# Graph network layers on one core: the attention layer's sum over edges as an inner loop of two groups, with a mask table of two groups

## What is computed

```
h = h @ W_lin + b_lin ; feat = (h @ W_gat).reshape(N, 8, 32)
el = sum(feat * attn_l, -1) ; er = sum(feat * attn_r, -1)
e = leaky_relu(el[src] + er[dst], 0.2)
m = segment_max(e, dst) ; e = exp(e - m[dst]) ; s = segment_sum(e, dst)
out = segment_sum(feat[src] * (e / s[dst])[:, :, None], dst)
```

## Time and profile before

| | us |
|---|---|
| median of 3 runs (4096.9 to 4102.8) | 4097.34 |
| the profiled execution's own time | 4102.93 |
| its span, first to last instruction | 4101.1 |
| PE busy (share of the span) | 2926.9 (71%) |
| DVE busy | 1751.3 (43%) |
| POOL busy | 1369.7 (33%) |
| ACT busy | 884.6 (22%) |
| PE products L2202, 832 rows | 232.1 |
| POOL gathers L1974, 416 | 406.9 |
| PE's mean granted clock, share of full speed | 0.849 |

### The profile page before, as it was taken

The page is one execution under the profiler, slowest core; times in us unless marked ns, Lnnn a source line. Parts: engine busy times, 40 slices in busy tenths (PEclk is TensorE's granted clock), DMA queues, the critical chain, the costliest instruction groups (busy, mean ns, idle before and its releaser), DMA issues. The chain is left out here.

```text
span 4101.1 us, 44629 instructions
## 1 busy us (share of the span) xinstructions
PE 2926.9 (71%) x13021; PEld 2101.9 (51%) x13087; DVE 1751.3 (43%) x4387; ACT 884.6 (22%) x1236; POOL 1369.7 (33%) x980
## 2 busy tenths in 40 slices
PE   2888779624344454779999979999999997434445
PEld 1455568423233333546666657989883443223334
DVE  5876445436556456733333314434343222111214
ACT  0246643100000000112222224444431221000000
POOL 2122200255554450037777740000000001666663
PEclk9999889756666667889999989999999999666767
DMA  1157875233332220122222227666743444333332
GB/s 56 61 201 248 289 263 163 86 93 87 95 94 87 81 82 26 39 78 74 74 74 74 77 67 264 199 210 206 267 133 112 141 141 140 93 91 92 91 90 88
DMA packets 325254, 504.89 MB, mean 123 GB/s; under 512 B 27225, under 2 KB 238877, under 8 KB 317005
## 3 DMA queue, kind: packets, MB, share of 16 engines
q1 hardware_dynamic: 284477, 391.28, 28.4%
q0 software_dynamic: 40672, 112.31, 9.9%
HBM read 351.56 MB, written 152.75 MB: 123 GB/s over the span
## 5 line engine op out<-in xcount | busy, mean ns | idle before, releaser
L1854 POOL DMA_INDIRECT e7got<-rel_d,rel_i x416 | 396.0, 952 | 1212.6 <-POOLq L2645 1013.8
L1974 POOL DMA_INDIRECT a_got<-feat_d,src_i x416 | 406.9, 978 | 594.3 <-POOLq L2303 238.6
L1488 PE MATMUL s_aggs<-s_blk_r,high 128*128 128x512 f32 (+1 forms) x1050 | 400.5, 381 | 21.0 <-DVE low L1607 20.8
L1488 PE MATMUL s_aggs<-s_blk_r,low 128*128 128x512 f32 (+1 forms) x1050 | 389.1, 371 | 0.0
L2686 PE MATMUL q_prods<-w,q_xt 128*128 128x512 f32 x800 | 352.6, 599 | 13.4 <-ACT q_xt L2706 13.4
L1890 PE MATMUL e7sums<-e7got,e7hot 128*128 128x256 f32 x832 | 257.7, 468 | 141.8 <-issue 121.8
L1706 POOL TENSOR_SCALAR g_absent<-g_pairs 128x3200 bf16<-128x3200 f32 x25 | 274.9, 10995 | 171.7 <-DMA g_pairs<-pairs_d 171.7
L1862 DVE TENSOR_SCALAR e7hot<-iota,dloc,weight 128x128 f32<-128x128 f32 x416 | 115.9, 364 | 480.1 <-DMA g_pairs<-pairs_d 356.7
L1753 PE MATMUL g_sums<-value,g_turned 128*128 128x257 f32 x1250 | 298.8, 383 | 8.6 <-ACT g_turned L1817 8.6
L1890 PEld LDWEIGHTS e7sums<-e7got,e7hot 128*128 128x128 f32 x832 | 195.7, 240 | 203.1 <-issue 168.7
L1731 PE MATMUL g_scores<-key_t,g_q 128*128 128x512 f32 (+1 forms) x700 | 280.4, 556 | 20.6 <-DMA g_q<-query_d 13.4
(11 more groups left out here) (416 smaller groups left out, 4513.2 us busy)
## 6 DMA issues: line engine op xcount, KB each, us to landing
s_blk<-turned_d SPq DMA_DIRECT2D x60, 1280.0 KB
rel_d<-q_rows SPq DMA_DIRECT2D x25, 2048.0 KB
s_blk<-turned_d SPq DMA_DIRECT2D x45, 960.0 KB
pairs_d<-u_rows SPq DMA_DIRECT2D x25, 1600.0 KB, 8.1
turned_d<-u_line SPq DMA_DIRECT2D x25, 1600.0 KB, 7.1
g_pairs<-pairs_d SPq DMA_DIRECT2D x25, 1600.0 KB, 6.8
t_blk<-pairs_d SPq DMA_DIRECT2D x20, 1280.0 KB
t_blk<-pairs_d SPq DMA_DIRECT2D x15, 960.0 KB
```

Source lines behind the costliest of these rows:

```text
L1488: last = pe.matmul(aggs[:, idx % 2, half, 0:w], feats[l][part][:, a, half * P:(half + 1) * P], blk_r[:, q % RINGS, a % GA, 0:w], start=a = ...
L1854: pool.indirect_dma_start(got[:, j % U, :], None, table, bass.IndirectOffsetOnAxis(ap=index[:, j:j + 1], axis=0)).then_inc(arrived[j % U / ...
L1974: pool.indirect_dma_start(got[:, n % 2, s, :], None, table, bass.IndirectOffsetOnAxis(ap=k.src_i[:, j:j + 1], axis=0)).then_inc(arrived[n ...
```

## The change

The eight groups of `total` become an inner loop on TensorE of four passes with two groups each. The group's word is loaded in the pass, just ahead of the group's waits, and the eight loads at the start of a chunk go. The slot of `got` is now addressed by a register. `hot` shrinks from 32 slots to 8, two groups, which are used in turn; so the mask of a group has to wait for the products of two groups earlier, not of the chunk before. `turn(n + 1)` moves from between groups 5 and 6 to behind group 7.

```diff
-        hot = sb("hot", [P, CS, P])
+        hot = sb("hot", [P, 8, P])
...
                 for g in range(NG):
-                    if n >= 1:
-                        dve.wait_ge(multiplied, (n - 1) * NG + g + 1)
-                    j = n * CS + 4 * g
-                    dve.tensor_tensor(hot[:, 4 * g:4 * g + 4, :], spreads[:, 256:256 + P].unsqueeze(1).broadcast_to([P, 4, P]),
+                    if n * NG + g >= 2:
+                        dve.wait_ge(multiplied, n * NG + g - 1)
+                    j, m = n * CS + 4 * g, 4 * (g % 2)
+                    dve.tensor_tensor(hot[:, m:m + 4, :], spreads[:, 256:256 + P].unsqueeze(1).broadcast_to([P, 4, P]),
                                       k.dloc[:, j:j + 4].unsqueeze(2).broadcast_to([P, 4, P]), ALU.is_equal).then_inc(made, 1)
...
-                def multiply(g, u):
-                    ins = pe.matmul(sums[:, 0:W], hot[:, 4 * g + u, :], got[:, b, 4 * g + u, :], start=False, stop=False)
-                    if u == 3:
-                        ins.then_inc(multiplied, 1)
-
-                for g in range(NG):
-                    if more and g == NG - 2:
-                        turn(n + 1, 1 - b)
-                    word = words[g]
-                    pe.wait_ge(made, n * NG + g + 1)
-                    pe.wait_ge(weighed, n * NG + g + 1)
-                    with pe.If((word & 15) == 0):
-                        for u in range(4):
-                            multiply(g, u)
...
+                def multiply(m, u, group):
+                    slot = (group * 4 + u).with_bounds(min_val=0, max_val=CS - 1)
+                    return pe.matmul(sums[:, 0:W], hot[:, 4 * m + u, :], tile_of(got[:, b, :, :], slot), start=False, stop=False)
+
+                with pe.Fori(0, NG // 2) as i:
+                    for m in range(2):
+                        g = i * 2 + m
+                        word = load_word(pe, k, (n * NG + g).with_bounds(min_val=0, max_val=S // 4 - 1))
+                        pe.wait_ge(made, n * NG + g + 1)
+                        pe.wait_ge(weighed, n * NG + g + 1)
+                        with pe.If((word & 15) == 0):
+                            for u in range(4):
+                                last = multiply(m, u, g)
+                            last.then_inc(multiplied, 1)
...
+                if more:
+                    turn(n + 1, 1 - b)
                 zeros(False).then_inc(closed, 1)
 
             def chunk(n, b, more):
-                words = [load_word(pe, k, n * NG + g) for g in range(NG)]
                 maximum(n, b, more)
-                total(n, b, more, words)
+                total(n, b, more)
```

More of the change, by code:

```diff
@@ L2192, in zeros, with total @@
                 return pe.matmul(sums[:, 0:W], k.zero_b[:, 0:P], k.zero_b[:, 0:W], start=start, stop=not start)
-            def total(n, b, more, words):
+            def total(n, b, more):
                 pe.wait_ge(resumed, n + 1)
@@ new lines, in total @@
+                with pe.Fori(0, NG // 2) as i:
[8 more added lines that the diff above has]
+                            last.then_inc(multiplied, 1)
+                        with pe.If((word & 15) != 0):
+                            for u in range(4):
+                                with pe.If(turn_here(word, u) != 0):
+                                    zeros(False).then_inc(full, 1)
+                                    pe.wait_ge(copied, tile_before(word, u) * 2 + 2)
+                                    zeros(True)
+                                last = multiply(m, u, g)
+                            last.then_inc(multiplied, 1)
```

## The result

The changed kernel takes 4166.62 us (median of 4 runs, 4157.39 to 4170.99), the kernel before 4100.07 us in the runs beside it (4 runs, 4096.90 to 4103.27): 1.0159 times the time, 95% interval 1.0139 to 1.0179, that is 66.5 us slower. The forecast was slower, by 45. The profiled execution took 4166.38 us with a span of 4164.6, 63.5 more than that of before.

The account below looks back on a forecast made before the run. Taken as the bound: waits for PE signals passed late during POOL's gather bursts. 37 + 27 = 64.0 us against 60.4 gave +40 over 11 chunks, chunks 11 and 12 +5: +45, 4142 us, range 4075 to 4225.

Parts of the forecast that it names:

- What bounds the kernel: Attention chunks with gathers: PE's signals pass late during POOL's bursts; nearly 19 us of waiting per chunk.
- Loads out of the start: Eight word loads, 5.1 us, leave each chunk's start; mostly free, a gain of 3.8 us once was taken.
- The mask's wait and late signals: DVE's masks wait for products two groups back; with late signals the scan comes 37 us after POOL's restart, against 32.2.
- Chunks 11 and 12: The last two attention chunks, without gathers beside them: +3 and +2 us, together +5.
- The loop: PE's inner loop: 39 branches back cost 8 us of sequencer time, already counted, without fetch stalls.
- R: Theory set up for the experiments: the loop's register steps cost the time; mask table and `turn`'s place don't matter.
- A: Rival, faster: early breaks in POOL's bursts bring the scan 25.2 us after restart; 4025 us, or 4064; chance 0.13.
- C: Rival, hardly a change: the burst's end releases the scan as now, 34.3 at most; 4097 to 4105 us; chance 0.15.
- D: Rival: each of 39 inner branches back stalls PE 4.7 us, +183, some hidden; 4280 us; chance 0.03.
- B: Rival, slower still: DVE hears of groups 4 and 5 only at the burst's end; 4201 to 4223 us; chance 0.24.

Follow-up runs that it names:

- e9: Kernel before with `turn` moved to the head of `total`, ahead of the carried sum: 4069.84 us, ratio 0.9976.
- e6: Pair, kernel before and changed kernel, both without three of every four gathers from chunk 2 on: 3733.40 us (0.9941) and 3834.48 us (1.0202).
- e0: Kernel before, unchanged, run once more for its trace on a second chip: 4083.14 us in one execution.
- e4: Kernel before with only the load of the word moved into the group: 4089.25 us, ratio 1.0022.
- e3: Kernel before with only `turn` moved behind group 7: 4129.24 us, ratio 1.0125.
- e2: Kernel before with only the mask table of two groups: 4101.09 us, ratio 1.0058.
- e1: Kernel before with two-group mask table, word load in the group and `turn` behind group 7, but no loop: 4121.96 us, ratio 1.0108.
- e5: Changed kernel with `turn` put back between groups 5 and 6, the last pass written out: 4132.51 us, ratio 1.0131 to the kernel before.
- e8: Changed kernel with a four-group mask table and two loop passes of four groups: 4146.45 us, ratio 1.0179 to the kernel before.
- e7: Kernel before with a POOL fill of some 2 us ahead of every fourth gather from chunk 2 on: 3896.68 us, ratio 1.0371.
- e11: Kernel before with `turn` at the head of `total` and word loads behind the last transposes of `maximum`: 3840.58 us, ratio 1.0221.

## Why the prediction was right, and where its size was off

*What bounds the kernel.* Right on this chip. That the signals pass late only in a burst fits e9 (given before the burst, the signal is there when DVE is ready) and a count of PE's slow sequencer rows (last section). On the third chip, without lateness, a chunk with gathers (39.8 us in e6) is even shorter than chunk 11. What was read as a property of the bursts is one of a burst and a chip together, and not of every burst: in the kernel before the signal of chunk 0 came through at 928.9, within the burst, and in e0's chunk 5 it was 2.2 us late in 32 gathers without a break. Whether the burst causes the lateness or only comes with it no run decides.

*Loads out of the start.* Right in size. In chunk 11 the stretch from the scan to the next carried sum shrank from 21.3 us (1582.31 to 1603.57) to 17.5 (1644.25 to 1661.71): the 3.8 us taken. In e4 it is 17.2. But e3, which keeps the loads at the start, has 17.5 as well: with `turn` last the scan comes late enough to hide them, so in the changed kernel their leaving can't be credited with the gain. And e4's chunk 11 as a whole wins 1.7 us (39.8), since the loads now stand between its products; its total is 0.2% slower.

*The mask's wait and late signals.* The mechanism held, and so did its size, in part by luck. The scan was put at 37 us and the rest of the chunk at 27, together 64.0; measured 38.8 and 26.1, together 64.9, so +4.5 us a chunk where +3.6 was forecast, 49 us in place of 40. Two steps inside were off. DVE's preparation was to end at 34 us and be hidden; it ends at 36.5, and in 7 of the 11 chunks, chunk 4 among them, it and not the transposes is what the scan follows (in the mean the transposes end 1.1 later). And POOL's burst does break for want of a signal, but for that of group 5, after 20 gathers in 8 of the 11 chunks (24 in two, 16 in one), where group 4's at 16 was taken; the signals are through 28.4 us after the restart in chunk 4 (1157.13 to 1185.54), not 24, and from there to the scan it is 8.2 us where 13 were costed. The two errors cancel, and that is luck.

*Chunks 11 and 12* are the term that was mis-sized: +9.4 and +7.2 us, 16.6 where 5 stood. The step that failed is the price of a group: "With prompt signals the round of two groups is" 4.1 us, "2.05 us a group", so 2 us more a chunk. Chunk 12 of the kernel after, PE:

```profile
1675.05 2.04 PE L2203 MATMUL a_sums<-a_got,a_hot 128*128 x8 [0.68 <-issue]
1678.10 1.30 PE L2203 MATMUL a_sums<-a_got,a_hot 128*128 x4 [1.01 <-DVE a_hot L2096]
1679.23 0.28 PE L2192 MATMUL a_sums<-zero_b 128*128 128x264 bf16 x1
1680.21 0.29 PE L2192 MATMUL a_sums<-zero_b 128*128 128x264 bf16 x1 [0.70 <-ACT den L2259]
1680.34 1.28 PE L2203 MATMUL a_sums<-a_got,a_hot 128*128 x4
1682.28 2.04 PE L2203 MATMUL a_sums<-a_got,a_hot 128*128 x8 [0.67 <-issue]
```

and before:

```profile
1613.04 4.79 PE L2202 MATMUL a_sums<-a_got,a_hot 128*128 128x264 f32 x20
1617.66 0.28 PE L2192 MATMUL a_sums<-zero_b 128*128 128x264 bf16 x1
1618.64 0.29 PE L2192 MATMUL a_sums<-zero_b 128*128 128x264 bf16 x1 [0.70 <-ACT den L2257]
```

One round of two groups, one of them with a closed sum, takes 1682.28 - 1675.05 = 7.23 us. I had left three things out. The closing of a sum and ACT's copy, 1.1 us, stand within the round now: DVE, which before could make all eight masks ahead of PE, waits through them. The two waits are in series: PE stands 1.01 us for the mask, after DVE stood for PE's products. And a group starts with some 0.67 us on issue, the word's load, which before stood at the start of the chunk. From the first product to the end, chunk 12's eight groups took 20.6 us before (1605.80 to 1626.37) and 27.6 after, 0.9 a group more where I had 0.25. In chunk 11 the transposes start 13.3 us later after the carried sum (32.4 against 19.1): 5.5 of it is the place of `turn`, which e3 has alone (24.5; 4.7 was costed), and 7.9 the slower groups, where 2 stood; the 3.8 go off. The kernels between split chunk 12: with the table alone it takes 26.2 us, +3.4 (e2), with the load in the group as well 26.6 (e1), with the loop and its register steps 30.0.

*The loop.* e1 to the kernel after adds the loop and its register steps; e2 to e5 adds the load in the group too, and e3 to e8 that and a table of four groups. Each costs 0.5 to 0.7% more, by ratios from different chips, each known to some 0.2%. That is 20 to 30 us, a third of the loss or somewhat more; R was right that far. The branches don't stall: the 52 of L2205 take 208 ns in the median, as the outer one did, 11 us of sequencer time together, and their greatest, 699, is of the size that other rows of PE's sequencer show in a burst. The rule of the Trainium skill ("Runtime: NRT & Kernel Launch", section "Instruction fetch mechanics"), that a taken branch out of the pages at hand stalls for its fetch, is not seen at work here; whether the start of the inner loop ever lies outside them no run tells.

*The rivals.* A fell: no chunk's scan came earlier than 36.5 us from the restart. C fell with it (34.3 at most), and D by the branches' 208 ns where it needed 4.7 us. B stayed a fragment: masks do wait 11.56 us within a burst, but when the burst breaks only one round is left, and the chunk comes out at 64.9 us and not at 70.

## What to carry to other kernels

A wait that is hidden behind another is not free to grow: the scan here takes the later of two inputs, and with the loop in place undoing either of them gave back 0.3% (e5) or nothing (e8) of 1.6, so look at both before undoing one. A double buffer of two makes every irregular delay of one side (a closed sum, a copy, a register load) part of the round; price a round with these delays in it, not by the mean of its busy times. And what hides or exposes such a loss may depend on the chip: the same edit cost 4.5 us a chunk where late signals covered part of it and 8.1 (with a quarter of the gathers) where none did.

## What the runs showed of the hardware

- The same kernel took 4078.37 us on one chip and 3756.04 on another, each within 0.6% between its runs. By the traces of e0 (first carried sum at 895.2, end of the layer at 1612.5, span 4081.4) and of e6's kernel before (850.2, 1353.4, 3728.5), 45 us of the 353 lie ahead of the attention layer's sums, 214 in them (a part of it from the gathers left out) and 94 behind.
- On the chips with lateness PE's sequencer rows come at some 700 or 1400 ns while POOL issues gathers back to back (a load at 1406 in the kernel before, register steps L2203 up to 1396 in the kernel after), and what they signal arrives late: 23 us in chunk 4 of the kernel before, 31.5 in chunk 0 of e3. In the attention layer the kernel before has 96 load, register and branch rows of 600 ns and more, the kernel after 132; every one starts within a burst of gathers or up to 3 us behind its end, none in chunks 11 and 12. Mostly the lateness clears within some 4 us of a break in POOL's burst. Not always: e3's chunk 0 was released only after a break of 2 us and four more gathers, and some signals came through within a burst. Whether the break is the cause is not settled (e7 was to tell). On the third chip there is no such row in the layer (e6, e7, e11), and no load over 0.32 us. Why chips differ in this wasn't tried.
- POOL's breaks of 0.7 to 7.7 us within a chunk lie only where a multiple of four gathers is done, the places at which it waits for PE; the 64 gathers of chunks 0 and 1 in the kernel before, which wait for nothing, and all bursts of 32 in e11 have none. So they are waits for PE's signals and no pauses of POOL's own.
